# A rewritten round order for an audio tower: position products ahead of the scores, value products in fours

## What is computed

```python
# tokenizer: frames of 100 samples -> power spectrum -> 40 mels -> 13 coefficients -> 192
mfcc = log(mel(power(fft(frames * window))) + 1e-6) @ dct.T
h = mfcc @ w_proj + b_proj
# attention on y = layernorm(h), h1 = rmsnorm(y) * norm1_w; 8 heads, 64 wide, values 24 wide
q, k, v = h1 @ wq, h1 @ wk, h1 @ wv
qr = einsum('bihn,ijn->bhij', einsum('bihd,hdn->bihn', q, w_pos), basis)   # relative positions, 32 functions
bias = (qr + uk + vr) * scale            # u.k and (v.w_pos).basis
attn = softmax(q k^T * scale + bias)
x = (attn @ v) @ wo + bo + y
x = gelu(rmsnorm(x) @ w1 + b1) @ w2 + b2 + x
h = h + x
# then h + expert layer on layernorm(h): 16 experts, each takes its 1000 best tokens
```

## Time and profile before

| | |
|---|---|
| time, median of 3 runs | 2250.64 us (2248.63 to 2255.05) |
| the profiled execution: time, span | 2256.45 us, 2254.7 us |
| granted TensorE clock, mean | 0.982 of full speed |
| busy: TensorE, weight loads, VectorE, ScalarE, GpSimd | 92%, 75%, 61%, 49%, 31% |

### The profile page before, as it was taken

How to read it: one execution, slowest core, us unless ns; L and a number is a source line. 1 busy time by engine, 2 the same in 40 slices (tenths; PEclk the granted TensorE clock), 3 DMA queues, 4 the chain that set the end, 5 groups by cost and what they waited for, 6 DMA issues and landing times. The chain is left out here.

```text
span 2254.7 us, 46810 instructions
## 1 busy us (share of the span) xinstructions
PE 2069.0 (92%) x13522; PEld 1700.7 (75%) x13522; DVE 1365.8 (61%) x3632; ACT 1103.7 (49%) x2680; POOL 704.0 (31%) x587
## 2 busy tenths in 40 slices
PE   2999999999999999999996699989999999999997
PEld 1677777777777777777774577778888888888886
DVE  1577767677776767677673577744555554555531
ACT  2677777767777777777763222122222222222221
POOL 0122122121212212121221000236665566665563
PEclk9899999999999999999997899999999999999998
DMA  5555655555555655555561633325454444454442
GB/s 142 156 146 147 168 143 163 148 158 151 151 163 144 167 147 155 150 156 161 143 165 50 161 103 102 93 54 89 91 97 77 73 78 88 91 98 76 73 80 31
DMA packets 317544, 272.43 MB, mean 121 GB/s; under 512 B 80740, under 2 KB 304822, under 8 KB 317494
## 3 DMA queue, kind: packets, MB, share of 16 engines
q1 hardware_dynamic: 238374, 235.01, 39.0%
q0 software_dynamic: 70656, 30.65, 9.6%
q10 hardware_dynamic: 8464, 6.15, 0.9%
HBM read 150.73 MB, written 120.54 MB: 120 GB/s over the span
## 5 line engine op out<-in xcount | busy, mean ns | idle before, releaser
L1134 POOL DMA_INDIRECT out<-ff_y,ff_idxs x128 | 261.8, 2045 | 245.5 <-DVE ff_y L1417 187.9
L1194 ACT ACTIVATE ff_sg<-ffp_g 128x500 f32<-128x500 f32 x192 | 112.9, 588 | 400.3 <-PE ffp_g L1529 369.9
L1121 POOL DMA_INDIRECT ff_xg<-xs_d,ff_idxg x128 | 205.1, 1603 | 297.1 <-issue 283.6
L468 ACT ACTIVATE sb_prob<-sb_ssb,sb_mx 125x250 f32<-125x250 f32 x512 | 253.1, 501 | 58.6 <-DVE sb_mx L562 58.6
L1541 PE MATMUL ffp_d<-ff_wd,ff_wide 128*125 128x192 f32 x1536 | 261.2, 327 | 16.0 <-DVE ff_wide L1404 15.2
L1404 DVE TENSOR_TENSOR ff_wide<-ff_sg,ffp_u 128x500 f32<-128x500 f32 x192 | 129.4, 674 | 221.1 <-PE ffp_u L1529 219.5
L1541 PEld LDWEIGHTS ffp_d<-ff_wd,ff_wide 128*125 128x125 f32 x1536 | 247.8, 188 | 19.9 <-issue 18.2
L1529 PE MATMUL ffp_g<-ff_xsp,ff_wsp 128*128 128x500 f32 x960 | 251.8, 392 | 1.6 <-DVE ff_xsp L1276 1.6
L1529 PE MATMUL ffp_u<-ff_xsp,ff_wsp 128*128 128x500 f32 x960 | 249.6, 390 | 0.0
L548 DVE COPY sb_ptsb<-ps_ptps 125x500 f32<-125x500 f32 x256 | 172.9, 675 | 123.8 <-PE ps_ptps L716 120.6
L1529 PEld LDWEIGHTS ffp_g<-ff_xsp,ff_wsp 128*128 128x128 f32 x960 | 180.2, 189 | 39.3 <-issue 2.7
(11 more groups left out here) (181 smaller groups left out, 3664.4 us busy)
## 6 DMA issues: line engine op xcount, KB each, us to landing
bias_d<-sb_rsb SPq DMA_DIRECT2D x256, 219.6 KB
sb_bsk<-bias_d SPq DMA_DIRECT2D x256, 218.8 KB
hx_d<-sb_hx SPq DMA_DIRECT2D x32, 336.0 KB
sb_hxl<-hx_d SPq DMA_DIRECT2D x32, 336.0 KB
ff_wd<-WdT SPq DMA_DIRECT2D x16, 576.0 KB
xs_d<-sb_xs SPq DMA_DIRECT2D x32, 238.0 KB
bias_d<-sb_rsb SPq DMA_DIRECT2D x256, 25.5 KB
sb_bsk<-bias_d SPq DMA_DIRECT2D x256, 25.4 KB
```

The source lines that it names most:

```text
L468: a.activation(prob[:, s % 2, t], ssb[:, s % 2, t], ACT.Exp, bias=mx[:, s % 2, t:t + 1], scale=-1.0, accum_out=rs[:, t, s:s + 1]).then_inc ...
L1121: g.indirect_dma_start(xg[:, t], None, xs_d[:, :], bass.IndirectOffsetOnAxis(idxg[:, t:t + 1], 0), bounds_check=last).then_inc(gat, 16)
L1134: g.indirect_dma_start(out_d[:, :], bass.IndirectOffsetOnAxis(idxs[:, t:t + 1], 0), y[:, t], None, bounds_check=last, compute_op=ALU.add). ...
```

## The change

The lists of all engines are written anew.
- The query weights are multiplied by the position weights once, at the start (`fold_mm`, from a new load `wqT`), and put beside the other weights as 256 more columns. The position queries of four heads then come straight from `hsp`, in slots 1 and 5 (five f32r matmuls each), instead of four float products from `qu`. Their copy to `qw` is four operations of 64 rows, twice a round, in place of one of 128 and one of 64 rows, four times.
- In an even slot the relative-position products of two heads stand in front of the scores.
- The DCT is folded into the projection (`wmel`); `logmel` goes straight into it, and the copy `mfcc` is gone.
- Value products go in groups of four heads (`quad_values`), after slot 3 (in slot 4) and in slot 0 of the next round; `ptsb` has four buffers.
- The inverse row sums are spread by true transposes.
- The third `w1` product goes to `tps` and no longer waits for the Gelu of the first two.
- `vtmp` is copied by VectorE, not ScalarE. `xnT` is copied in slot 1, after `qw`; `x1` in slot 3; token statistics in slot 4, ahead of the low part of `h2sp`. The switch back to the exponential's table moves from behind the Ln and the Gelu to slots 4 and 6, in front of the exponentials and behind the `rsb` copies. The store of `scT` and the sum `xb` of GpSimd move to slot 4.

```diff
-        QK_USE = [0, 4, 10, 14]
-        QW_USE = [1, 5, 11, 15]
-        V_USE = [6, 7]
-        R_USE = [2, 3, 8, 9, 12, 13, 16, 17]
+        QK_USE = [0, 4, 9, 13]
+        QW_USE = [1, 10]
+        QW_SLOT = {1: 0, 5: 1}
+        V_USE = [5, 6]
+        R_USE = [2, 3, 7, 8, 11, 12, 14, 15]
...
@@ ScalarE
+                    if bt is not None and s == 4 or bc is not None and s == 6:
+                        tables_stale = True
...
                             a.activation(rsb[:, h % 2], bank2(qps[R_USE[h] % 2], NDE, TP)[:, :, 0:ND], ACT.Copy).then_inc(q_ev[R_USE[h] % 2], 2)
+                    if tables_stale:
+                        a.preload_act_table_set(EXP_SET)
...
-                        a.activation(mfcc[0:MFCC], tps[0:MFCC, 0:FRAMES], ACT.Copy).then_inc(t_ev, 1)
...
@@ VectorE
+                    if bq is not None and s in QW_SLOT:
+                        use = QW_USE[QW_SLOT[s]]
+                        done = 4 * bq + 2 * QW_SLOT[s]
+                        halves = slice(0, 64), slice(64, 128)
+                        dve.wait_ge(q_mm, Q_USES * bq + use + 1)
+                        for i in range(2):
+                            p = 2 * QW_SLOT[s] + i
+                            v.tensor_scalar(qw[halves[i], i], qps[use % 2][halves[i], 0:FRAMES], cq[halves[i], p:p + 1], None, ALU.add).then_inc(qw_hi, 1)
+                        for i in range(2):
+                            p = 2 * QW_SLOT[s] + i
+                            dve.wait_ge(qw_hi, done + i + 1)
+                            v.scalar_tensor_tensor(out=qw[halves[1 - i], i], in0=qps[use % 2][halves[i], 0:FRAMES], scalar=cq[halves[i], p:p + 1],
+                                                   in1=qw[halves[i], i].bitcast(F32), op0=ALU.add, op1=ALU.subtract).then_inc(q_ev[use % 2], 1)
...
+                    if s > 0:
+                        pt_copy(bb_, s - 1)
+                    if bq is not None and s == 3:
+                        for t in range(NT):
...
+                            v.tensor_copy(vtmp[:, t], qps[V_USE[t] % 2][0:TP, 0:D]).then_inc(q_ev[V_USE[t] % 2], 2)
+                    if bd is not None and s == 1:
+                        dve.wait_ge(d_mm, D_USES * bd + 1)
+                        wait(dve, c_st, 80 * bd)
+                        v.tensor_copy(xnT[:], bank2(cps, FRAMES, KD)).then_inc(d_ev, 1)
...
@@ TensorE
-            def pair_values(b, p):
+            def quad_values(b, k):
 
                 if b is not None:
-                    h = 2 * p
-                    if h % QUAD == 0:
-                        pe.wait_ge(vz_in, 2 * b + 1 + h // QUAD)
-                    if h == 0:
+                    pe.wait_ge(vz_in, 2 * b + 1 + k)
+                    if k == 0:
                         wait(pe, ot_ev, b)
-                    pe.wait_ge(pt_ev, HEADS * b + h + 2)
+                    pe.wait_ge(pt_ev, HEADS * b + QUAD * (k + 1))
                     for j in range(NT):
-                        for i in range(2):
-                            c = VC * ((h + i) % QUAD)
-                            ins = m(otps[c:c + VC, h // QUAD], vz[:, j, h + i], ptsb[:, i, j], start=j == 0, stop=j == NT - 1)
+                        for i in range(QUAD):
+                            ins = m(otps[VC * i:VC * i + VC, k], vz[:, j, QUAD * k + i], ptsb[:, i, j], start=j == 0, stop=j == NT - 1)
...
+                    if bq is not None and s in QW_SLOT:
+                        use = QW_USE[QW_SLOT[s]]
+                        q_freed(pe, bq, use)
+                        col = ALL_COLS + 128 * QW_SLOT[s]
+                        for k, (wk, xp, xk) in enumerate(PARTS):
+                            ins = m(qps[use % 2][:, 0:FRAMES], wsp[:, wk, col:col + 128], hsp[:, xp, xk], start=k == 0, stop=k == len(PARTS) - 1)
+                        ins.then_inc(q_mm, 1)
                     br, pair = biases(s, bq, bb_)
                     if br is not None:
...
+                    if bb_ is not None and s % 2 == 0:
+                        pair_scores(bb_, s // 2)
```

More of the change, by code:

```diff
@@ L49 @@
 ALL_COLS = 2 * HEADS * DK + D + DFF
+POS_COLS = HEADS * N_POS
 SROW = 2 * 128 + EXPERTS
@@ new lines, in body @@
+                    if bc is not None and s == 7:
+                        b0 = D_CHAIN * bc
+                        dve.wait_ge(c_mm, C_USES * bc + 5)
+                        dve.wait_ge(c_xb, bc + 1)
+                        wait(dve, c_st, 80 * bc)
+                        v.tensor_tensor(h1[:], bank2(cps, D, TP), xb[:], ALU.add).then_inc(c_ev, 1)
+                        dve.wait_ge(c_ev, C_USES * bc + 5)
+                        for t in range(NT):
+                            v.bn_stats(c_stats[:, t], h1[:, t]).then_inc(d_ch, 1)
+                        apart(dve, READY, (d_ch, b0 + 2))
+                        for t in range(NT):
+                            v.bn_aggr(c_mv[:, t], c_stats[:, t]).then_inc(d_ch, 1)
+                        dve.wait_ge(d_ch, b0 + 4)
+                        v.tensor_scalar(d_v[:], c_mv[:, :, 1], EPS, None, ALU.add).then_inc(d_ch, 1)
@@ L667, in body @@
                         ins.then_inc(t_ev, 1)
+                    if bc is not None and s == 7:
+                        b0 = D_CHAIN * bc
+                        dve.wait_ge(d_ch, b0 + 6)
+                        for t in range(NT):
+                            v.tensor_scalar(xs[:, t, 0:D], h1[:, t], c_mv[:, t, 0:1], d_y[:, t:t + 1], ALU.subtract, ALU.mult).then_inc(d_ch, 1)
             rounds(dve, body)
@@ L792, in body @@
-                    if bc is not None and s == 5:
-                        pe.wait_ge(c_ev, C_USES * bc + 2)
-                        ps = bank2(cps, FRAMES, 128)
-                        for j in range(2):
-                            col = COLS["w1"][0] + j * 128
-                            for k, (wk, xp, xk) in enumerate(PARTS):
-                                ins = m(ps[:, j], wsp[:, wk, col:col + 128], h2sp[:, xp, xk], start=k == 0, stop=k == len(PARTS) - 1)
-                        ins.then_inc(c_mm, 1)
@@ new lines, in body @@
+                    if bq is not None and s == 4:
+                        qk(bq, 2)
+                    if bc is not None and s == 4:
+                        if bd is not None:
+                            pe.wait_ge(d_ev, D_USES * bd + 3)
+                        pe.wait_ge(c_ch, C_CHAIN * bc + C_CHAIN)
+                        pe.wait_ge(c_ev, C_USES * bc + 1)
+                        transposes(bank2(cps, FRAMES, 128), h2n, c_mm)
+                    if s == 4:
+                        quad_values(bb_, 0)
@@ new lines, in body @@
+                    if bc is not None and s == 5:
+                        pe.wait_ge(c_ev, C_USES * bc + 2)
+                        ps = bank2(cps, FRAMES, 128)
+                        for j in range(DFF // 128):
+                            col = COLS["w1"][0] + j * 128
+                            if j == 2 and bt is not None:
+                                pe.wait_ge(t_ev, T_USES * bt + 3)
+                            for k, (wk, xp, xk) in enumerate(PARTS):
+                                ins = m(ps[:, j] if j < 2 else tps[:, 0:FRAMES], wsp[:, wk, col:col + 128], h2sp[:, xp, xk], start=k == 0, stop=k == len(PARTS) - 1)
+                            if j > 0:
+                                ins.then_inc(c_mm, 1)
```

360 lines of the change are left out of this document (163 added, 197 removed).

## The result

The changed kernel takes 2,293.33 us (median of 4 runs, 2,289.66 to 2,302.26) against 2,252.85 us for the kernel before (4 runs): a ratio of 1.0187, with an interval of 1.0151 to 1.0223. It is 40.5 us slower; the prediction was 25 us faster, and 2,293 us lies above its range. The profiled execution has a span of 2,293.5 us against 2,254.7, and a mean granted TensorE clock of 0.954 of full speed against 0.982.

The account below looks back on a forecast made before the run. TensorE's list bounds the tower now, and a chain across engines of 35.2 us a round replaces it. 28 rounds x -0.75 = -21, with +3 -4 -3, gives -25 us from the median: 2,226 us, range 2,170 to 2,270.

Parts of the forecast that it names:

- chain sum: One full tower round followed from engine to engine in six steps: 35.2 us, with TensorE idle for 4.5.
- the 2.1 us stall: Slot 1: TensorE's gate product stands 2.1 us for `xnT`, which VectorE copies only after `qw`.
- step 1: From the gate product in slot 1 to `x1` in slot 3, through products, scores, transposes, mel, q/k and `wo`: 6.33 us.
- step 2: ScalarE and VectorE in slots 3 to 5, from `x1` over two table loads, statistics and `h2sp` to `qw`: 12.0 us.
- 3, `h1`: Slot 6: TensorE's position products, scores, transposes, q/k and `w2` products up to VectorE's `h1`: 5.74 us.
- 4, the value group of slot 0: VectorE in slots 7 and 0, from `h1` and its statistics to the last `ptsb` copy: 5.31 us.
- 5, the first `qw` operation: TensorE in slot 0: value group, transposes and the new query product, up to VectorE: 2.96 us.
- step 6: VectorE in slot 1: four `qw` operations, a `ptsb` copy and `xnT`, then the gate product: 2.87 us.
- The rival for this: VectorE's `qw` blocks in slots 1 and 5 are slower: 36.15 us a round, even; at 0.65 each, 2,267 us; chance 0.20.
- Four heads abreast: Slot 0 value group forecast at 1.0 us; rival, not abreast: 0.94 more, 36.2 a round, 2,253 us, chance 0.14.
- switches of table: ScalarE's two table switches on the path cost another 1.38 us each: 38.0 a round, 2,304 us; chance 0.02.
- The shorter chain: Tower rounds: the chain's ends overlap and TensorE's list of 30.7 us binds: 2,099 us, or 2,165; chance 0.10.

Follow-up runs that it names:

- experiment 1: Changed kernel with the spectrum product of slot 1 issued six times instead of once, filling TensorE's wait for `xnT`: 2,246.69 us, 0.9956 of the kernel before.
- 11: Kernel before with `xnT` copied late, in slot 1 behind `otsb`, and five extra spectrum products ahead of the gate product: 2,329.9 us, 1.0321.
- experiment 2: Changed kernel with VectorE's copy of `xnT` put ahead of `qw` in slot 1: 2,173.85 us, 0.9628 of the kernel before.
- 6: Changed kernel with `xnT` copied ahead of `qw` and the scores back ahead of the position products in even slots: 2,147.66 us, 0.9522 of the kernel before.
- 5: Changed kernel with `xnT` copied ahead of `qw`, and the low part of `h2sp` ahead of the statistics in slot 4: 2,266.75 us, 1.0048 of the kernel before.
- 12: Changed kernel with `xnT` first, scores first, high parts of `qw` on ScalarE, and low `h2sp` ahead of the statistics: 2,175.77 us, 0.9641 of the kernel before.
- 8: Changed kernel with `xnT` copied ahead of `qw` and the high parts of `qw` copied by ScalarE: 2,145.41 us, 0.9508 of the kernel before.
- 9: Changed kernel with `xnT` first, scores first and the high parts of `qw` copied by ScalarE: 2,142.87 us, 0.9496 of the kernel before.
- experiment 4: Kernel before with the position products of two heads put in front of the scores in each even slot: 2,420.97 us, 1.0729.

## Why the prediction was wrong

**The step that failed is the chain sum, where every term is taken at full clock.** "The sum is 6.33 + 12.0 + 5.74 + 5.31 + 2.96 + 2.87 = 35.2 us a round, with TensorE idle for 4.5 of it." The terms right behind the 2.1 us stall, relative-position products, scores and transposes in the 6.33, were read from rows of a round with a clock of 1.00, in which TensorE waits for 1.4 us in all. The forecast put a wait in front of them longer than any in that round, and left their durations as they were. By the prediction's own six steps, from the traces at about 600 us, in us:

| step, up to the start of | forecast | wait filled (experiment 1) | changed kernel |
|---|---|---|---|
| 1, `x1` (from the gate product) | 6.33 | 6.52 | 8.06, in long rounds 9.65 |
| 2, the position products of slot 6 | 12.0 | 12.24 | 12.24 |
| 3, `h1` | 5.74 | 5.65 | 5.65 |
| 4, the value group of slot 0 | 5.31 | 5.13 | 5.13 |
| 5, the first `qw` operation | 2.96 | 2.67 | 2.67 |
| 6, the gate product | 2.87 | 3.35 | 3.35 |

Only step 1 differs between the two kernels. The low clock cost 37.61 - 35.55 = 2.06 us a round, 58 us over 28 rounds. Experiments 1 and 11 show this as cause: filled with useless work, the same wait leaves the clock at 1.00.

The Trainium skill, "TensorE: Matmul & The Clock Gate", Part 1 (HAM oscillation), describes this pattern for a kernel that waits for transfers: each wait lets the clock fall and the next stretch starts slow, over and over. In the skill's kernel the waits last 3 to 5 us. The trace agrees with the pattern and not with the length: here waits of 1.94 to 2.48 us for VectorE are enough. The prediction did not weigh that rule and had no rival for it.

**The rest of the chain stood.** At full clock it is 35.55 us against 35.2, inside the 34.6 to 35.75 given. That is 0.42 less than before, 12 us in the 28 rounds (forecast 21), and experiment 1 is 10 us faster over all. That the sum is so close is in part luck: steps 1, 2 and 6 are 0.91 longer than added up, and steps 3 to 5 are 0.56 shorter.
- `qw`, in steps 2 and 6: "three pitches of 0.39 (that of the two `hsp` operations) and 0.48" was mis-sized. All four go at 0.50 to 0.51, so a block costs 2.03 instead of 1.56 or 1.65. The rival for this priced it at +0.9 a round if every operation waits for its neighbour; the pitch came out as that rival has it, and step 6 is 0.48 longer and step 2 is 0.24. Its figure for a pitch of 0.65 is too low: eight operations slower by 0.14 add 1.1 to its 36.15, 37.3 and not 36.7.
- The gate product: "it stands for 2.1", measured 2.36. The cause named, `xnT` queued behind `qw`, was right, and worth more than its own length: experiment 2 takes 2.1 us off the full-clock chain and 4.2 off the round as it was.
- Four heads abreast: 1.0 us, so that rival is gone. Of the switches of table nothing beyond the load shows: the Gelu's load starts at 652.67 and the Gelu at 653.97. That rival is gone too.
- The shorter chain did not come: VectorE's order binds, as argued against it.
- The prologue cost 3.3 (forecast 3). The drain gave back 6.2 up to the experts' first matmul (forecast 3). Of the 4 us forecast for the first rounds 0.6 came: by the third spectrum product (75.61 us before, 75.97 after) they had given back nearly 3, but by the first `otsb` that was gone. From 92.4 to 99.0 us, on the way there, the granted clock is 0.50, where before it was 1.00; what it cost there was not measured.

**What the change is worth by its parts.** With the wait for `xnT` gone the new lists are 3.7% faster than the old, and 5% with one of the two edits for `qw`. The new order of products and scores is a small loss at full clock (0.77 us a round, 6 against 2). None of the folded weights, four-head groups and true transposes was taken back alone, so their shares of the 5% stay open.

## What to carry to other kernels

When a sum of the chain puts a wait of about 2 us in front of TensorE, its matmuls behind the wait can't be priced by rows from a round without such waits: count up to twice their time for some 3 us, or fill the wait with work, even useless work. An operation whose input is long ready and for which TensorE waits goes to the front of VectorE's list. A move that shortens one wait is to be followed to the next wait on the same engine, since experiments 5 and 12 only moved the waiting, and in 5 the clock fell behind the new wait.

## What was not expected of the hardware

- TensorE's clock is at 1.2 GHz for some 3 us, at times about twice that, behind waits of 1.94, 2.36 and 2.48 us. Behind a wait of 1.94 us it fell in 24 rounds of 28, behind one of 2.48 us in 25 of 28, and behind 2.36 us in all 28. What decides in which rounds it stays up was not tested. Waits up to 1.14 us alone in their stretch left it at 2.4 GHz (experiments 6, 8 and 9), and so did the 0.66 and 1.27 us of experiment 12, which have 2.4 us of work between them; but in experiment 4 it fell behind one of 1.23 us, with 0.8 us of work between it and one of 0.72.
- So identical rounds have unequal lengths (37.1 and 38.67 us). That pattern by itself is a sign to look at the granted clock.
- VectorE's `qw` operations of 64 rows by 250 from PSUM started every 0.50 us; the one of 128 rows lasted 0.47, with the next start 0.51 behind the earlier trace rows. Half the rows saved nothing, and whether an operation depends on its neighbour made no difference.
